# Rows of 15 small embedding tables for the first group: from GpSimd's gathers to TensorE products with ones and zeros

## What is computed

```python
e = jnp.stack([tbl_0[ids[:, 0]], ..., tbl_38[ids[:, 38]]], axis=1)      # (2048, 39, 16)
# three layers; h and k run over fields (or over the maps of the layer before), s over 128 maps
z = relu(einsum('bhd,bkd,hks->bsd', x0, xk, W) + b)
# half of the maps of layers 0 and 1 go on as xk, the rest and layer 2 are summed over d
h = relu(concat([z, dense_ctx]) @ W_top1 + b_top1); h = relu(h @ W_top2 + b_top2); y = h @ W_top3
```

## Time and profile before

| | us |
|---|---|
| median of 3 runs | 2489.73 (2489.48 to 2490.6) |
| the profiled execution, its own time | 2490.02 |
| its span in the trace | 2488.2 |
| PE busy | 2399.6, 96% of the span |
| DVE busy | 2240.9, 90% |
| POOL busy | 1679.1, 67% |
| ACT busy | 1058.4, 43% |

### The profile page before, as it was taken

How to read it: one execution, slowest core, us unless ns; L and a number is a source line. 1 busy time by engine, 2 the same in 40 slices (tenths; PEclk the granted TensorE clock), 3 DMA queues, 4 the chain that set the end, 5 groups by cost and what they waited for, 6 DMA issues and landing times. The chain is left out here.

```text
span 2488.2 us, 29429 instructions
## 1 busy us (share of the span) xinstructions
PE 2399.6 (96%) x7702; PEld 1442.7 (58%) x7702; DVE 2240.9 (90%) x1657; ACT 1058.4 (43%) x1053; POOL 1679.1 (67%) x1059
## 2 busy tenths in 40 slices
PE   0899999999999999999999999999999999999989
PEld 0465555665565666556556655656665555665556
DVE  0799998999999999999999999999999998999993
ACT  0244443444444444444444444443444443444445
POOL 7877766767677676777767677776768767544340
PEclk9999999999999999999999999999999999999999
DMA  6888787998778789888779887888988777888730
GB/s 162 203 197 196 193 191 183 208 215 191 190 199 191 196 212 213 189 190 199 191 196 216 207 190 187 201 192 197 215 210 188 192 197 173 210 205 195 182 79 11
DMA packets 172546, 469.79 MB, mean 189 GB/s; under 512 B 28987, under 2 KB 63163, under 8 KB 172245
## 3 DMA queue, kind: packets, MB, share of 16 engines
q1 hardware_dynamic: 148869, 461.35, 76.7%
q0 software_dynamic: 19968, 5.15, 2.2%
q10 hardware_dynamic: 3680, 2.95, 0.5%
HBM read 457.02 MB, written 12.33 MB: 189 GB/s over the span
## 5 line engine op out<-in xcount | busy, mean ns | idle before, releaser
L638 POOL TENSOR_TENSOR low<-prod,high 128x1024 fp32r<-128x1024 f32 x384 | 945.9, 2473 | 553.7 <-ACT high L801 551.2
L914 DVE TENSOR_TENSOR prod<-spread,maps 128x2048 f32<-128x2048 f32 x448 | 1016.7, 2281 | 72.8 <-ACT direct L743 20.9
L801 ACT ACTIVATE high<-prod 128x1024 fp32r<-128x1024 f32 (+1 forms) x576 | 596.2, 1056 | 715.9 <-DVE prod L914 458.4
L616 POOL DMA_INDIRECT landed<-in_tbl,rows_id x585 | 620.6, 1061 | 165.6 <-issue 148.6
L1014 PE MATMUL zacc_a<-prod,w_plain 128*128 128x512 f32 (+1 forms) x1536 | 709.1, 596 | 17.0 <-DVE prod L899 11.1
L1014 PE MATMUL zacc_b<-prod,w_plain 128*128 128x512 f32 (+1 forms) x1536 | 706.2, 594 | 5.9 <-DVE prod L914 5.9
L1014 PEld LDWEIGHTS zacc_a<-prod,w_plain 128*128 128x128 f32 (+1 forms) x1536 | 291.9, 190 | 288.9 <-issue 259.9
L1014 PEld LDWEIGHTS zacc_b<-prod,w_plain 128*128 128x128 f32 (+1 forms) x1536 | 291.2, 190 | 275.0 <-issue 246.8
L899 DVE TENSOR_TENSOR prod<-shifted,x_thrice 117x1024 f32<-117x1024 f32 x224 | 266.7, 1230 | 66.8 <-DMA shifted<-x_periods 53.7
L1049 PE MATMUL zacc_b<-low,w_high 128*128 128x512 f32 x672 | 281.2, 499 | 6.2 <-POOL low L638 6.2
L1049 PE MATMUL zacc_a<-low,w_high 128*128 128x512 f32 x672 | 280.7, 498 | 0.7 <-DVE low L869 0.5
(11 more groups left out here) (103 smaller groups left out, 1618.9 us busy)
## 6 DMA issues: line engine op xcount, KB each, us to landing
spread<-x_periods SPq DMA_DIRECT2D x608, 512.0 KB, 16.5
shifted<-x_periods SPq DMA_DIRECT2D x188, 468.0 KB
x_thrice<-x_periods SPq DMA_DIRECT2D x93, 156.0 KB
shifted<-x_periods SPq DMA_DIRECT2D x64, 156.0 KB
landed<-in_tbl,rows_id POOLq DMA_INDIRECT x585, 4.6
spread<-x_periods SPq DMA_DIRECT2D x32, 256.0 KB, 20.7
x_periods<-x SPq DMA_DIRECT2D x30, 256.0 KB, 2.2
spread<-features SPq DMA_DIRECT2D x4, 512.0 KB, 4.6
```

What stands on the lines that cost most here:

```text
L616: nc.gpsimd.indirect_dma_start(out=landed[:, f, :], out_offset=None, in_=tables[f], in_offset=bass.IndirectOffsetOnAxis(ap=rows[:, f:f + 1 ...
L638: nc.gpsimd.tensor_tensor(low[0:rows, at_, :], prod[0:rows, at_, :], high[0:rows, slot(j, SPLIT, NH), :], ALU.subtract).then_inc(s_lowp, 1)
L801: nc.scalar.activation(high[0:rows, h, :], made(turn, j)[0:rows, :], ACT.Copy).then_inc(s_round, 1)
L914: nc.vector.tensor_tensor(prod[:, at_:at_ + 2, :], spread[:, t:t + 2, :], maps[:, :].unsqueeze(1).to_broadcast([128, 2, COLS]), ALU.mult). ...
```

## The change

Fifteen of the tables with 1,000 or 1,250 rows are no longer gathered for the first group. Such a table is loaded whole: 125 partitions hold 8 (or 10) rows each (ACT's queue, 15 loads of 62.5 or 78 KB). SP loads the 128 ids of each of the 15 fields, repeated on 125 partitions (960 KB), and small row numbers. DVE compares ids and row numbers: for each table one instruction gives 125 x 8 x 128 (or 125 x 10 x 128) ones and zeros. PE then multiplies: 8 (or 10) matmuls per table, each with a 125 x 128 piece of ones and zeros as weights and 125 x 16 of the table as the moving operand, added up in PSUM. ACT copies the 128 x 16 result into `landed`. The other 24 fields are gathered as before, and the transpositions wait for both. All groups after the first are unchanged.

```diff
+FOUND = [{0: 8, 2: 10, 5: 8, 6: 8}, {12: 8}, {16: 8, 17: 8, 19: 8, 21: 10, 23: 10}, {25: 8, 28: 8, 31: 8}, {34: 8, 38: 8}]
+FOUND_ROWS, HOT, HITS, TEN_AT = 125, 5, 6, 8
...
             sp.dma_start(rows_id[:, :], ids[0:ROWS, :]).then_inc(s_first, 16)
+            sp.dma_start(sought, a["ids_first"].unsqueeze(0).to_broadcast([FOUND_ROWS, len(FOUND_ORDER), ROWS])
+                         ).then_inc(s_numbers, 16)
+            sp.dma_start(row_no, a["row_no"]).then_inc(s_numbers, 16)
...
-            sp.dma_start(parts_in[:, 0:plan_r - PARTED0, :], a["w_parted"]).then_inc(s_parts, 16)
...
+            sp.dma_start(parts_in[:, 0:plan_r - PARTED0, :], a["w_parted"]).then_inc(s_parts, 16)
...
                     for q, fields in enumerate(BLOCKS):
-                        gather(fields[0], fields[-1] + 1, s_first_g[q])
+                        for f in fields:
+                            if f not in FOUND[q]:
+                                gather(f, f + 1, s_first_g[q])
...
+            def copy_found(f):
+
+                act.wait_ge(s_hit, FOUND_ORDER.index(f) + 1)
+                nc.scalar.activation(landed[:, f, :], hit_of(f), ACT.Copy).then_inc(s_found, 1)
+
+            for n, f in enumerate(FOUND_ORDER):
+                act.dma_start(kept_rows[f], a[f"tbl_{f}"].rearrange("(p c) d -> p c d", c=parts_of(f))).then_inc(s_table[n], 16)
...
             for q in range(TURNED):
+                for f in FOUND[q]:
+                    copy_found(f)
+                if q == 2:
+                    act.wait_ge(s_parts, 16)
+                    nc.scalar.activation(w_high[:, 0:parts12, :], parts_in[:, 0:parts12, :], ACT.Copy).then_inc(s_cast, 1)
                 copy_block(q)
...
-            dve.wait_ge(s_first_g[-1], 16 * len(BLOCKS[-1]))
+            dve.wait_ge(s_numbers, 32)
+            for n, f in enumerate(FOUND_ORDER):
+                c = parts_of(f)
+                ten = TEN_AT if c == 10 else 0
+                if n >= HOT:
+                    dve.wait_ge(s_hit, n - HOT + 1)
+                nc.vector.tensor_tensor(hot_of(f), sought[:, n, :].unsqueeze(1).to_broadcast([FOUND_ROWS, c, ROWS]),
+                                        row_no[:, ten:ten + c].unsqueeze(2).to_broadcast([FOUND_ROWS, c, ROWS]),
+                                        ALU.is_equal).then_inc(s_hot, 1)
...
+            def find(f):
+
+                n, c = FOUND_ORDER.index(f), parts_of(f)
+                pe.wait_ge(s_table[n], 16)
+                pe.wait_ge(s_hot, n + 1)
+                if n >= HITS:
+                    pe.wait_ge(s_found, n - HITS + 1)
+                for i in range(c):
+                    done = nc.tensor.matmul(hit_of(f), hot_of(f)[:, i, :], kept_rows[f][:, i, :], start=i == 0, stop=i == c - 1)
+                done.then_inc(s_hit, 1)
+
             def turn_first():
 
                 for q in range(TURNED):
-                    pe.wait_ge(s_first_g[q], 16 * len(BLOCKS[q]))
+                    for f in FOUND[q]:
+                        find(f)
+                    pe.wait_ge(s_first_g[q], 16 * (len(BLOCKS[q]) - len(FOUND[q])))
+                    pe.wait_ge(s_found, found(q))
```

More of the change, by code:

```diff
@@ L72 @@
 BLOCKS = [range(FIELDS)[128 // DIM * q:128 // DIM * (q + 1)] for q in range(TURNED)]
+FOUND = [{0: 8, 2: 10, 5: 8, 6: 8}, {12: 8}, {16: 8, 17: 8, 19: 8, 21: 10, 23: 10}, {25: 8, 28: 8, 31: 8}, {34: 8, 38: 8}]
+FOUND_ORDER = [f for block in FOUND for f in block]
+FOUND_ROWS, HOT, HITS, TEN_AT = 125, 5, 6, 8
+HOT_AT = 6
 OFFSET, AFTER = 3, 12
@@ L121, with found, parts_of @@
 PARTED0 = N0 - PLAIN0
+def found(q):
+    return sum(len(block) for block in FOUND[:q + 1])
+def parts_of(f):
+    return next(block[f] for block in FOUND if f in block)
 def weight_slot(j):
@@ L276, in build @@
         s_first_t = sem("s_first_t")
+        s_numbers = sem("s_numbers")
+        s_table = [sem(f"s_table{f}") for f in FOUND_ORDER]
+        s_hot = sem("s_hot")
+        s_hit = sem("s_hit")
+        s_found = sem("s_found")
         s_first_x = sem("s_first_x")
@@ L397, in build, with hot_of, hit_of @@
         assert plan_r * MAPS <= 4 * COLS and N0 * MAPS <= COLS
+        hot_at = HOT_AT * COLS
+        sought = staged[0:FOUND_ROWS, hot_at:hot_at + len(FOUND_ORDER) * ROWS].bitcast(i32).rearrange("p (n b) -> p n b", b=ROWS)
+        hot_at += len(FOUND_ORDER) * ROWS
+        row_no = staged[0:FOUND_ROWS, hot_at:hot_at + TEN_AT + 10].bitcast(i32)
+        hot_at += TEN_AT + 10
+        kept_rows = {}
+        for f in FOUND_ORDER:
+            kept_rows[f] = staged[0:FOUND_ROWS, hot_at:hot_at + parts_of(f) * DIM].rearrange("p (c d) -> p c d", d=DIM)
+            hot_at += parts_of(f) * DIM
+        hot = [staged[0:FOUND_ROWS, hot_at + 10 * ROWS * i:hot_at + 10 * ROWS * (i + 1)] for i in range(HOT)]
+        assert hot_at + 10 * ROWS * HOT <= N1 * COLS
+        def hot_of(f):
+            c = parts_of(f)
+            return hot[FOUND_ORDER.index(f) % HOT][:, 0:c * ROWS].rearrange("p (c b) -> p c b", b=ROWS)
+        def hit_of(f):
+            n = FOUND_ORDER.index(f) % HITS
+            return (maps1, *zacc)[n // 2][:, n % 2 * BANK:n % 2 * BANK + DIM]
         at = [0]
@@ L484, in _ @@
             sp.dma_start(rows_id[:, :], ids[0:ROWS, :]).then_inc(s_first, 16)
+            sp.dma_start(sought, a["ids_first"].unsqueeze(0).to_broadcast([FOUND_ROWS, len(FOUND_ORDER), ROWS])
+                         ).then_inc(s_numbers, 16)
+            sp.dma_start(row_no, a["row_no"]).then_inc(s_numbers, 16)
+            sp.dma_start(ident[:, :], a["ident"]).then_inc(s_const, 16)
             sp.dma_start(all_ids[:, :, :], ids.rearrange("(g p) f -> p g f", p=ROWS)).then_inc(s_all, 16)
-            sp.dma_start(ident[:, :], a["ident"]).then_inc(s_const, 16)
-            sp.dma_start(parts_in[:, 0:plan_r - PARTED0, :], a["w_parted"]).then_inc(s_parts, 16)
             sp.dma_start(w_plain[0:TRIPLE, plan_f - PLAIN0:plan_f, :], a["w0_ab"][:, 0:PLAIN0, :]).then_inc(s_w0, 16)
@@ L1154, in laid_out @@
 def laid_out(given):
+    ids = np.asarray(given["ids"])
+    given["ids_first"] = np.ascontiguousarray(ids[0:ROWS, FOUND_ORDER].T)
+    given["row_no"] = np.concatenate([np.arange(FOUND_ROWS * c, dtype=np.int32).reshape(FOUND_ROWS, c) for c in (8, 10)], axis=1)
     def take(name, dtype=np.float32):
```

2 lines of the change are left out of this document (removed).

## The result

The changed kernel takes 2522.9 us (median; 2521.1 to 2523.5) against 2489.5 us for the kernel before in the same comparison: a ratio of 1.0134, 95% interval 1.0121 to 1.0146, so 33 us slower. One of its five launches was in a slow state, at 5127.4 us, and stands in neither the spread nor the ratio. The forecast was slower by 25 us, 2514.6, in a range of 2489 to 2522; the direction was right and the time lies just above the range.

What follows compares the result with a forecast made beforehand. PE was taken to bound the kernel, with the start hanging on the last transposition: 24.2 + 52.9 + 3.5 = 80.6 us, 24.9 later than before, so 2490.0 + 24.9 = 2514.9, median 2514.6 us; range 2489 to 2522.

Steps and rivals of the forecast that it cites:

- What ends last: First group: PE's products end last, last transposition at 80.6 against 55.65; its shift of 24.9 us is the time's shift.
- PE begins at 17.2 + 7 = 24.2 (bounds 20.5 and 26.8): PE's first product waits for constants behind 1.99 MB of added loads, taken as 7 us more.
- A pass costs 0.21 us: PE's products: each pass costs one 128-column weight load, 0.21 us at half clock; 252 passes make 52.9 us.
- half level throughout: PE stays at 1.2 GHz during all products; 2510 to 2522 us, chance 0.62.
- five closings: Block ends on PE: standing still for ACT's last copy and semaphores, 0.7 us x 5 = 3.5 us.
- DVE and ACT covered: DVE's comparisons (19.4 us, from some 6 us on) and ACT's copies (4 us) hide behind PE's products.
- GpSimd's 18.8 us: POOL, first group: fifteen gathers fewer at 1.25 us each would bring the gathered side's last transposition to 36.9.
- the first rival: Full-clock products on PE, including 0 to 4 us for loads delaying the next block's write; 2490 to 2496, chance 0.21.
- Full clock: PE's clock rises during the products, 0.11 us a pass; last transposition at 57.6, say 2494 us, chance 0.21.
- clock in part: PE's clock rises in block 2 and falls in pauses, half the passes at each level; 2500 to 2508, chance 0.08.
- hidden loads: PE's short loads overlap, a pass nears 0.03 us and gathers decide; 18.8 us earlier, 2471, chance 0.09.
- Break-even at 0.111 us a pass: PE's products: the pass price at which the last transposition would start at 55.65, as before.

Runs made afterwards that it cites:

- e1_cut: The changed kernel with its transfers to 125 partitions (ids, row numbers, 15 tables) each cut into 112 and 13 partitions; 2516.8 us, ratio 1.0121.
- e3: The changed kernel with transfers cut into 112 and 13 partitions and the loads of biases and small ahead of the weights; 2500.6 us, ratio 1.0053.
- e5_eight: The changed kernel with cut transfers and early constants, but 8 of the 15 tables found by products and 31 gathered; 2488.2 us, ratio 0.9990.
- e12: Eight tables by products, one block ahead, constants early, transfers cut, first three pieces of spread loaded behind x_thrice and shifted; 2499.6 us, ratio 0.9971 on slower chips.
- e4_warm: The changed kernel with 32 matmuls of 512 columns on zeros in front of the products; 2518.1 us, ratio 1.0122.
- e2_consts: The changed kernel with the loads of biases and small moved ahead of all weights in SyncE's queue; 2506.7 us, ratio 1.0077.
- e7_left_out: The changed kernel without the 15 tables (rows set to zero, reference not computed), 24 gathers, constants early; 2479.1 us, ratio 0.9960.
- e6_single: The changed kernel with cut transfers, early constants and one-pass float32r products, table rows split into rounded and remainder parts; 2498.9 us, ratio 1.0034.
- e10_ahead: Eight tables by products, made one block ahead, 31 gathered, constants early, transfers cut; 2500.3 us, ratio 0.9975 on slower chips.
- e11_single_twelve: One-pass float32r products for 12 tables, one block ahead, early rounding, remainders prepared block by block, cut transfers, early constants; 2512.2 us, ratio 1.0010 on slower chips.

## Why the prediction was right in direction and wrong in size

- **What ends last.** Right. The start of the last transposition sets the time: it moved by 33.3 us, layer 1 by 33.8, the span by 32.5, the median by 33.4. Across the change and e1 to e3 the shift of the last transposition (33.3, 27.8, 17.3, 11.9) and of the median (33, 30, 20, 14) go together within 3 us. It does not hold as a rule: in e5 to e12 the chain behind the last transposition took 32 to 45 us.
- **"PE begins at 17.2 + 7 = 24.2 (bounds 20.5 and 26.8)."** This is the step that failed. It came at 32.2, 8 us later, and those 8 us are the miss of the time (2522.9 for 2514.6). The sum took bytes at the rate of the earlier trace rows and packets at the price of the earlier trace rows, and so assumed that all 16 DMA engines would serve them. The runs showed engines busy for 66% at 150 GB/s instead. The rows of before hold no transfer to 125 partitions. e1_cut, same bytes in other shapes, starts at 26.6, inside the bounds: 5.6 of the 8 us are the shape, and the other 2.4 lie between the value chosen and the upper bound. The upper bound should have allowed for a transfer that uses part of the engines; it was a bound on the amount, not on the rate.
- **"A pass costs 0.21 us", half level throughout.** Right: 0.213 measured, with 333 ns loads in every stretch of the products, and e4_warm shows that it is not a matter of how PE comes in. 252 x 0.213 is 53.7, which leaves 0.6 us for each of five closings where 0.7 was taken; together 56.7 us against 56.4.
- **DVE and ACT covered.** Right in the price (1.22 us for 1024 elements, 1.50 for 1280, as integers). DVE started at 13.5 and not at 6, for the same reason as above; it did not bind. ACT did not bind in the change either, but it issued tables until 29 us, and with the constants early (e2_consts) that cost PE 1.2 us.
- **GpSimd's 18.8 us.** The gathers' side was never last, so it did not enter the sum, but the price was too high as a term. In the change the 24th gather was issued at 34.5 and not at 31.7; taken alone (e7_left_out) the start gained 11.4 us: 3.2 went to one long gather, 1.2 to a later landing and 3.0 to later loads of `x_thrice`. The forecast has no term for these; the first rival alone had 0 to 4 us for loads that delay the next block's write.
- **The rivals.** Full clock, clock in part and hidden loads fell with the 0.213 us a pass in the change, and e4_warm took away the defence that PE only never came in at the full level. Break-even at 0.111 us a pass was the right question: the pass cost twice that.
- **The range.** Its end, 2522, cut off part of the case it belonged to (2525 by the text's own bounds), so a time of 2522.9 would have been inside that case though not for its reason: the start lay beyond its own bound, and the pass at its low end.

## What to carry to other kernels

In these runs a gather by products of ones and zeros cost one weight load of 128 columns per 125 rows of the table and pass, the same with 16 and with 32 columns behind it: 0.21 us at the half clock, twice that for plain float32, so 3.4 us for a table of 1,000 rows against 1.25 us of a gather on GpSimd. It can pay only for as many tables as TensorE gets done while GpSimd is at the others; eight of them, started early, made no difference, fifteen cost time. Before new work is put on an idle engine, look at the wait that stands ahead of it in the queue (here three constants behind all the weights, 17 us), and at how many DMA engines a transfer of a new shape keeps busy.

## What the runs showed of the hardware that was not expected

- 15 loads of 62 to 78 KB to 125 partitions and one of 940 KB kept the DMA engines half idle (share 0.50, 139 GB/s from 8 to 16 us) and blocked the issuing engines, 11 us for one issue on SP and 28 us for 15 on ACT. Cut into 112 and 13 partitions, the same bytes let the first product start 5.6 us sooner.
- A stream of passes of 128-column loads with 16 columns each counts as busy in the profile (55.0 of 56.7 us) and yet was at the half clock from 37 us on when it began at the full one (e4_warm: loads of 190 ns up to 36 us, of 333 ns from 37 on), and did not rise again in 23 us.
- From the last block's write to the loads of `x_thrice` it was 3.0 us before, 6.6 in e7_left_out and 12.5 in e6_single, where the blocks follow each other more closely. In e6_single SP's own issues for earlier blocks stand in between; in e7_left_out the cause is not separated.
- One gather of 2.8 to 4.0 us on POOL in place of 0.94 stands in the first 80 us of each of the 14 profiles (3.96 at 56.71 in before, 3.95 at 23.13 in e7_left_out, 3.56 at 33.93 in e5_eight). Its cause is open.
- On two of the chips the kernel before took 2507 us instead of 2489, and in two profiles from one of them engines stand for 7 to 13 us in the first 95 us with nothing in the trace that ends it: ACT in e10_ahead, and PE, DVE and ACT together in e11_single_twelve. What these pauses are stays open.
